# Four transformer layers on one core: the quantised layer's feed-forward in pieces over three attentions, and unread identity products on TensorE

## The chip, the cores and the metric

The kernel runs on one NeuronCore of one Trainium2 chip. The metric is the device time of one execution, in microseconds (us). Two kernels are compared by the median of their runs.

## The reference, cut to what matters

A batch of 16 sequences of 128 tokens with 256 features goes through four layers, one after the other. All arithmetic is in fp32 apart from the quantised products. Layer 1 is the one that the change touches:

```
def layer1(x, context):                       # 16 heads of 16 features, D = 256
    h1 = ln(x);  x = attn(h1, h1)      + x    # _attn below, deltas d_*1
    h2 = ln(x);  x = attn(h2, context) + x    # deltas d_*2
    h3 = ln(x);  a, g = split(h3 @ ff_w1 + ff_b1)          # ff_w1: 256 x 2048
    return a * gelu(g) @ ff_w2 + ff_b2 + x                 # ff_w2: 1024 x 256

def _attn(x, ctx):                            # fq: round to 8 bits, clip, scale back
    q, k, v = heads(x @ wq), heads(ctx @ wk), heads(ctx @ wv)
    attn = softmax(fq(q) @ fq(k).T * SCALE)
    return merge(fq(attn) @ fq(v)) @ wo + bo
```

Layer 0 has an attention over features and a feed-forward, layers 2 and 3 have two masked or plain attentions and a feed-forward each.

## The kernel before, in words

The 16 sequences are taken in four groups of four (g = 0 to 3). A group has two streams (st = 0, 1) of two sequences each. While one stream is in its attention, the other stream's projections, norms and feed-forward are issued between the steps of that attention. Every engine has its own in-order program; all are written out by the same planner, so the order on an engine is the order in the planner's lists.

An attention of a stream is 8 units of 4 heads x 128 queries x 128 keys. Function `attend` calls `together`, which runs 13 steps. In the quantised layer step i issues, on TensorE (PE): the score product of unit i (line 804, bf16, 512 columns), then the four transposes of unit i-4 (`turn`, line 816), then the value products of unit i-5 (`values`, line 831). VectorE (DVE) takes the row maxima of a unit's scores (lines 1191, 1193), ScalarE (ACT) the four exponentials (line 985), GpSimd (POOL) weighs and rounds them (line 1390); the transposed unit is copied back by DVE (units 0 to 3, line 1215) or ACT (units 4 to 7, line 976). Scores of unit u wait for the exponentials of unit u-2, because they share one of two PSUM banks; the transposes of unit u wait for POOL's rounding of it.

Each other piece of work has a slot, a step number, and is issued on PE right after that step's attention work; on the other engines one step later. The pieces of a stream in layer 1 are: `y` and `sum` (output projection and residual), `norm`, `scale`, `tin` (norm of x, transposed; ACT copies it to hT), `k`, `q`, `v` (projections: 4 matmuls each, then three DVE instructions that quantise, lines 1007, 1009, 1013), `keys` (POOL, line 1309), and the feed-forward: `f0` to `f7`, each 4 matmuls for one 128-wide chunk of both halves of ff_w1, a Gelu on ACT (line 942) and a product on DVE (line 1089) that writes a chunk of `hid`; then `y2`, 16 matmuls over `hid`, and `sum`. An fp32 matmul of the program is two records of the trace. PSUM banks 6 (`one`) and 7 (`other`) serve all these pieces; `f` alternates between them.

One pass of layer 1 runs four attentions: stream 1's first, stream 0's second, stream 1's second, stream 0's first of the next group. `joined_pass` puts the whole feed-forward of stream 0 into the third and that of stream 1 into the fourth, two chunks to a slot, with `y2` after them and the next group's `k`, `q`, `v` after `y2`. The slots run past the 13 steps, so these two attentions last longer than the other two. They are called the long attentions below, the others the short ones. Layers 0 and 1 use `joined_pass`, layers 2 and 3 `ahead_pass`.

Of the kernel before, what the change touches and what calls it, by code (L numbers as in the profile page):

```python
# [8 lines left out]
ACT = mybir.ActivationFunctionType  # L9
# [5 lines left out]
P = 128  # L15
C = D // P
G = 2
# [153 lines left out]
AHEAD_SLOT = {"stage": 0, "scale": 0, "ctx": 3, "tin": 3, "bias": 4, "k": 5, "q": 5, "v": 6, "keys": 10}  # L171
FIRST_AHEAD = 2
CLOSING_SLOT = {"ot": 0, "y": 1, "sum": 1, "norm": 2, "scale": 3, "post": 5, "tin": 7, "bias": 8}
LEFT_SLOT = {"sum": 1, "norm": 2, "scale": 4, "post": 6}
# [65 lines left out]
def program(nc, a, out):  # L240
    ctx = ExitStack()
    with ctx:
# [167 lines left out]
        def passes(eng, emit_mix, emit_piece, late, before_last=lambda layer: None):  # L410
# [31 lines left out]
            def joined_pass(layer, g, after, left):  # L442
# [10 lines left out]
                return left  # L453

            def ahead_pass(layer, g, after, left):
# [20 lines left out]
            left = []  # L476
            for layer in range(FIRST_AHEAD):
                for g in range(NG - 1):
                    left = joined_pass(layer, g, (layer, g + 1), left)
                before_last(layer)  # L480
                left = joined_pass(layer, NG - 1, (layer + 1, 0), left)
            for layer in range(FIRST_AHEAD, NL):
# [69 lines left out]
        LATE = 1  # L552
        SUM_LAG = 1
        KEYS_AHEAD = 3
        LOCAL_STEPS = {
# [28 lines left out]
        def _(pe):  # L584
# [12 lines left out]
            def emit_piece(layer, g, st, ahead=False, shift={}):  # L597
# [11 lines left out]

                def emit(piece, arg, n):  # L610
                    swapped = ahead or "early" in arg
                    if piece == "ctx":
                        if st == 1:

                            pe.wait_ge(c[0]["yadd_done"], G * use("yadd", layer, g, 0))
                        pe.wait_ge(q["ctx_loaded"], 16 * (use("ctx", layer, g, 0) + 1))
                        turned(one, ctx_in[st]).then_inc(q["ctx_ps"], 1)
# [138 lines left out]
            def emit_mix(kind, layer, g, st, arg, n, mix):  # L756
# [51 lines left out]
                def turn(u):  # L808
                    if quant:
                        pe.wait_ge(s["rounded"], U * phase("qatt", layer, g, mix, st) + u + 1)  # L810
                    else:
                        pe.wait_ge(s["exp_ready"], U * ap + u + 1)

                    pe.wait_ge(s["PT_ready"], U * ap + u - 1)
# [58 lines left out]
        def _(act):  # L873
            def emit_piece(layer, g, st, ahead=False, shift={}):
                q = c[st]
                due = partial(use_shifted, shift)
                target = hT_ahead[st] if ahead else hT[st]

                def emit(piece, arg, n):
                    swapped = ahead or "early" in arg  # L880
                    if piece == "ctx":
                        act.wait_ge(q["ctx_ps"], use("ctx", layer, g, 0) + 1)
                        act.activation(cT[st].rearrange("p c t -> p (c t)"), one, ACT.Copy).then_inc(q["ctx_ready"], 1)
                    elif piece == "stage":
# [10 lines left out]
                    elif piece == "tin":  # L895
                        act.wait_ge(q["tin_ps"], due("tin", layer, g, n["tin"]) + 1)
                        for m in range(C):
                            if arg:
# [33 lines left out]
                    elif piece[0] == "f":  # L932
                        f = int(piece[1:])
                        k = use("ffn", layer, g, n["ffn"])
                        b = one if f % 2 == 0 else other
                        if arg["act"] == "geglu":
# [63 lines left out]
        def _(dve):  # L1000
            def emit_piece(layer, g, st, ahead=False, shift={}):
# [12 lines left out]

                def emit(piece, arg, n):
                    swapped = ahead or "early" in arg
                    if piece == "norm":
                        k = due("norm", layer, g, n["norm"])

                        if n["yadd"]:  # L1020
                            dve.wait_ge(q["yadd_done"], G * use("yadd", layer, g, n["yadd"]))
                        else:
                            dve.wait_ge(q["yadd_done"], G * use("yadd", layer - 1, g + 1, 0))
# [17 lines left out]
                    elif piece == "sum":  # L1041
                        b = one if "act" in arg else other
                        dve.wait_ge(q["y_ps"], use("yadd", layer, g, n["yadd"]))
                        if "res" in arg:
# [17 lines left out]
                    elif piece in ("q", "k", "v") and "quant" in arg:  # L1062
# [4 lines left out]
                        if piece == "v":  # L1067
                            quantise(Vzb[st].rearrange("p g a x d -> p (g a) x d")[:, :, 0:4:3, :],
                                     O[st].rearrange("p g d -> p (g d)"), one if swapped else other, d, at, q["v_ready"], G)
                        else:  # L1070
                            dst, scratch, b = (QTb[st], QT[st], other if swapped else one) if piece == "q" else (KTb[st], KT[st], one if swapped else other)
                            quantise(dst.rearrange("p c t -> p (c t)"), scratch.rearrange("p c t -> p (c t)"), b, d, at,
                                     q[piece + "_ready"], C)
# [11 lines left out]
                    elif piece[0] == "f" and arg["act"] == "geglu":  # L1085
                        f = int(piece[1:])
                        b = one if f % 2 == 0 else other
                        dve.wait_ge(q["gate_ready"], FC * use("geglu", layer, g, 0) + f + 1)
# [380 lines left out]
```

## Time and profile before

| | |
|---|---|
| median of 3 runs | 1998.0 us (1997.23 to 1998.41) |
| profiled execution: its time | 2000.4 us |
| profiled execution: its span | 1998.7 us |
| PE / DVE / ACT / POOL busy | 1801.4 / 1275.4 / 1043.4 / 906.9 us |
| mean granted TensorE clock | 0.929 of 2.4 GHz |
| layer 1 from its second attention to layer 2's first score product | 357.6 to 933.2 us |

The page gives, for the slowest core, each engine's busy time over the span, and a strip in 40 slices with the busy tenths and the clock that TensorE was granted. A stretch can be asked for by itself; so can the chain of waits, which is followed back from the last instruction: at each step to what released it, or to the instruction before it on the same engine. Busy times of matmuls are modelled and overlap, so the distance from one start to the next, or the chain, says what a run of them costs.

### The profile page before, as it was taken

To read this page: it belongs to the slowest core of one execution; us is meant where nothing else is said; L and a number is where in the kernel's file an instruction comes from. 1 tells how busy PE (TensorE), PEld (TensorE's weight loads), DVE (VectorE), ACT (ScalarE), POOL (GpSimd) and SP (SyncE) were. 2 spreads that over 40 slices of the span, in tenths; PEclk is the share of its full clock that TensorE was granted. 3 is DMA by queue.
4 is the path that set the end of the run, shared out by engine and by line. 5 is a ranking of instruction groups with operands and counts; after the bars stand their busy time and mean duration, and the time that the engine had idled before them with its cause. 6 is when DMAs were issued, how large, how long until landed. Compare 5 with 4: busy or idle time off the path is not lost.

```text
span 1998.7 us, 34297 instructions
## 1 busy us (share of the span) xinstructions
PE 1801.4 (90%) x12225; PEld 1334.7 (67%) x12225; DVE 1275.4 (64%) x2286; ACT 1043.4 (52%) x3078; POOL 906.9 (45%) x1209
## 2 busy tenths in 40 slices
PE   4999888799889889889999999999999999999997
PEld 4787766466566656657767677676676676766766
DVE  5899996765665575574575756856646538365471
ACT  2222224565565475465565565655545656565662
POOL 5466555654463464463254444644444333333340
PEclk8999988788878878879999999999999999999999
DMA  7200000002000000000002000000000000000000
GB/s 228 92 10 6 11 6 6 1 6 90 1 6 6 1 6 6 1 6 6 1 7 90 1 7 6 6 7 1 7 6 2 12 1 7 22 7 1 12 1 11
DMA packets 31071, 35.63 MB, mean 18 GB/s; under 512 B 3164, under 2 KB 29752, under 8 KB 30520
## 3 DMA queue, kind: packets, MB, share of 16 engines
q1 hardware_dynamic: 30904, 33.44, 5.2%
q8 instruction: 100, 1.64, 0.3%
q14 instruction: 67, 0.55, 0.1%
HBM read 31.34 MB, written 2.10 MB: 17 GB/s over the span
## 4 chain that ended last, share of the span: by engine, by line
PE 59%; DVE 20%; ACT 11%; issue 6%; SPq 2%; DMA 1%; POOL 1%; DVEq 0%; ACTq 0%; POOLq 0%
PE ps L594 31%; PE ps L806 6%; PE ps L744 6%; PE ps L816 5%; PE ps L850 4%; ACT work L985 4%; DVE xn L1039 3%; ACT work L992 3%; DVE work L1185 3%; PE ps L607 2%; DVE rowmax L1189 2%; PE ps L766 1%; ACT hT L899 1%; DVE O L1228 1%; PE ps L831 1%
## 5 line engine op out<-in xcount | busy, mean ns | idle before, releaser
L594 PE MATMUL ps<-hT,w_slot 128*128 128x256 f32 x1696 | 413.7, 398 | 16.7 <-ACT hT L899 16.2
L1314 POOL TENSOR_TENSOR work<-KT,own_head 128x512 f32<-128x512 f32 x256 | 262.4, 1046 | 286.7 <-PE ps L806 179.7
L594 PEld LDWEIGHTS ps<-hT,w_slot 128*128 128x128 f32 x1696 | 326.2, 198 | 77.9 <-ACT hT L899 22.0
L992 ACT ACTIVATE work<-work,rowmax 128x128 f32<-128x128 f32 x768 | 246.1, 394 | 167.2 <-DVE rowmax L1189 166.5
L816 PEld LDWEIGHTS ps<-ident,work 128*128 128x128 f32 x1536 | 199.7, 153 | 170.6 <-issue 89.5
L985 ACT ACTIVATE work<-ps,rowmax,score_scale 128x128 f32<-128x128 f32 x512 | 228.7, 478 | 132.5 <-DVE rowmax L1193 132.0
L816 PE MATMUL ps<-ident,work 128*128 128x128 f32 x1536 | 266.3, 302 | 18.0 <-ACT work L992 17.2
L806 PE MATMUL ps<-work,QT 128*128 128x512 f32 x512 | 266.5, 605 | 9.9 <-POOL work L1314 4.9
L1390 POOL TENSOR_SCALAR work<-work,winv 128x128 f32<-128x128 f32 x512 | 185.5, 382 | 155.3 <-DVE winv L1205 153.1
L1228 DVE RECIPROCAL O<-ps 128x128 f32<-128x128 f32 x128 | 122.2, 955 | 176.4 <-PE ps L850 175.7
L978 ACT ACTIVATE work<-ps 128x512 f32<-128x512 f32 x256 | 151.0, 597 | 91.1 <-PE ps L816 90.4
L1330 POOL TENSOR_SCALAR vareps<-meanvar 128x2 f32<-128x2 f32 x88 | 19.4, 221 | 384.2 <-DVE meanvar L1032 381.1
L1061 DVE TENSOR_TENSOR x_all<-ps,x_all 128x512 f32<-128x512 f32 x72 | 49.6, 690 | 148.6 <-PE ps L594 83.9
L947 ACT ACTIVATE hid<-ps,vcols 128x256 f32<-128x256 f32 x192 | 80.8, 472 | 106.9 <-PE ps L594 106.7
L1189 DVE TENSOR_REDUCE rowmax<-work 128x4 f32<-128x512 f32 x192 | 131.7, 686 | 6.6
L1039 DVE TENSOR_SCALAR xn<-x_all,meanvar,rstd 128x256 f32<-128x256 f32 x176 | 128.5, 770 | 3.0 <-POOL rstd L1332 1.9
L1309 POOL TENSOR_TENSOR work<-QKb,own_quad 128x512 bf16<-128x512 bf16 x64 | 70.7, 1124 | 131.4 <-issue 125.8
L804 PE MATMUL ps<-work,QKb 64*128 64x512 bf16 x128 | 64.7, 511 | 63.7 <-ACT work L985 45.5
L594 PE MATMUL ps<-w_slot,OT 128*128 128x256 f32 x448 | 115.6, 404 | 6.0 <-ACT OT L931 4.8
L744 PE MATMUL ps<-w_slot,hid 128*128 128x256 f32 x512 | 116.5, 381 | 1.7 <-ACT hid L947 0.9
L985 ACT ACTIVATION_READ_ACCUMULATOR work<-ps,rowmax,score_scale 128x1 f32 x512 | 115.0, 225 | 0.0
L594 PE MATMUL ps<-w_slot,hid 128*128 128x256 f32 x512 | 113.2, 379 | 0.0
(132 smaller groups left out, 3112.0 us busy)
## 6 DMA issues: line engine op xcount, KB each, us to landing
ctx_in<-in_ctx SPq DMA_DIRECT2D x32, 256.0 KB, 2.7
w_slot<-in_L_xattn_W SPq DMA_DIRECT2D x2, 1024.0 KB, 6.3
w_slot<-in_L_xattn_ff_w SPq DMA_DIRECT2D x1, 2048.0 KB, 11.6
w_slot<-in_L_xattn_ffn_w SPq DMA_DIRECT2D x2, 1024.0 KB, 9.4
w_slot<-in_L_xattn_w SPq DMA_DIRECT2D x2, 1024.0 KB, 9.9
out<-x_all SPq DMA_DIRECT2D x8, 256.0 KB, 2.1
x_all<-in_x SPq DMA_DIRECT2D x1, 1536.0 KB, 12.9
pad<-in_mask_Bx1x1xS_fk SPq DMA_DIRECT2D x1, 1024.0 KB, 6.4
```

The lines of the kernel that those rows point to most:

```text
L594: mm = pe.matmul(dst, lhsT(k), rhs(k), start=(k == 0 and not onto), stop=(k == chunks - 1 and not more))
L744: mm = pe.matmul(one[:, j * D:(j + 1) * D], hid[:, k, tok(j)], w[arg["w2"]][:, k, :], start=(k == 0), stop=(k == FC - 1))
L806: pe.matmul(bank(u % 2), QT[st][:, m, tok(j)], KB[u % NK], start=True, stop=True).then_inc(s["scores_ps"], 1)
L816: mm = pe.transpose(bank(2 + u % 2)[:, tok(h)], prob[u % (NP if quant else NPF)][:, tok(h)], ident[:, :])
L978: act.activation(PTF[u % 4], bank(2 + u % 2), ACT.Copy).then_inc(s["PT_ready"], 1)
L985: ex = act.activation(prob[i % NP][:, tok(h)], bank(i % 2)[:, tok(h)], ACT.Exp, bias=shifts[:, at:at + 1], scale=score_scale[:, arg["quant ...
L992: ex = act.activation(prob[i % NPF][:, tok(h)], src[:, tok(h)], ACT.Exp, bias=shifts[:, at:at + 1])
L1039: dve.tensor_scalar(xn[st][:, j, :].unsqueeze(1), x_of(g, st, j), meanvar[st][:, j, 0:1], rstd[st][:, j:j + 1], ALU.subtract, ALU.mult).th ...
L1189: dve.tensor_reduce(shift_u, sc, AX.X, ALU.max, negate=True).then_inc(s["shift_ready"], 1)
L1228: dve.reciprocal(oinv[st][quarter], bank(4 + m)[:, sums_at:sums_at + S]).then_inc(s["oinv_ready"], 1)
L1314: pool.tensor_tensor(KB[u % NK].rearrange("p (h k) -> p h k", h=HU), keys, own_head[:, e:HC:2].unsqueeze(2).broadcast_to([P, HU, S]), ALU. ...
L1390: w = pool.tensor_scalar(prob[u % NP][:, tok(h)], prob[u % NP][:, tok(h)], winv[:, u // 2 % 2, at:at + 1], MAGIC, ALU.mult, ALU.add)
```

## The change: two edits

1. Layer 1 gets a pass of its own, `spread_pass`. The feed-forward of a stream is no longer in one attention. Its chunks f0 to f3 stand in one attention (slots 8 to 11, one to a slot), f4 to f7 in the next, and the 16 matmuls of `y2`, in four parts, at slots 0 to 3 of the third, with their `sum` at slot 4. The chunks use bank 6 alone, so a chunk's matmuls wait until DVE has read the chunk before; `k`, `q`, `v`, `tin` and `ctx` use bank 7 alone, so `q` waits for the quantised `k` and `v` for the quantised `q`. The next group's `k`, `q`, `v` stand at slots 7, 8, 9, inside the 13 steps. The last group of layer 1 keeps the joined form for its own feed-forward, and takes over what group 2 has left.
2. In every attention of layer 1 PE issues products of the identity with itself (`warm`, 128x128, fp32) into the PSUM bank of the next transposes, which nothing reads: 3, 6, 6 ahead of the score products of units 2, 3, 4, and 2, 3, 3, 3 ahead of the transposes of units 0 to 3. These are 26 per attention.

```diff
+SPREAD_START = {"tin": 3, "ctx": 4, "bias": 4, "k": 7, "q": 8, "v": 9, "keys": 9}
+SPREAD_NORM = {"norm": 8, "scale": 10}
+SPREAD_CLOSING = {"ot": 0, "y": 1, "sum": 1, "norm": 2, "scale": 4, "tin": 6, "bias": 8}
+SPREAD_HIDDEN = 8
+SPREAD_SUM = 4
+def spread_closing(layer):
+    hidden = [(SPREAD_HIDDEN + int(piece[1:]) % (FC // 2), piece, arg, n) ... if piece[0] == "f"]
+    product = [(part, f"y2{part}", pieces[y2][2], pieces[y2][3]) for part in range(Y2)]
+    return chain, hidden[:FC // 2], hidden[FC // 2:], product
...
+            def spread_pass(layer, g, after, left):
+                into_a, into_b, into_c = left
+                attend(layer, g, 1, 0, middle(0) + into_a)
+                if after[0] != layer:
+                    attend(layer, g, 0, 1, middle(1) + into_b)
+                    pieces, later = joined(layer, g, after, 0)
+                    attend(layer, g, 1, 1, [(p[0] // 2 if p[2] != "sum" else 1,) + p[1:] for p in into_c] + pieces)
+                    pieces, _ = joined(layer, g, after, 1)
+                    attend(*after, 0, 0, pieces + later)
+                    return []
+                attend(layer, g, 0, 1, middle(1) + start(0, SPREAD_NORM) + into_b)
+                chain_0, first_0, second_0, product_0 = end(0)
+                attend(layer, g, 1, 1, chain_0 + start(0, SPREAD_START) + first_0 + start(1, SPREAD_NORM) + into_c)
+                chain_1, first_1, second_1, product_1 = end(1)
+                attend(*after, 0, 0, chain_1 + start(1, SPREAD_START) + second_0)
+                return product_0 + first_1, second_1, product_1
...
+        WARM_SCORES = {2: 3, 3: 6, 4: 6}
+        WARM_TURNS = {0: 2, 1: 3, 2: 3, 3: 3}
...
+                    elif spread and piece in ("k", "q", "v"):
...
+                            pe.wait_ge(q["k_ready" if piece == "q" else "q_ready"], C * (use("att", layer, g, n["att"]) + 1))
...
+                    elif spread and piece[0] == "f":
...
+                            pe.wait_ge(q["hid_ready"], FC * use("ffn", layer, g, n["ffn"]) + f)
+                        product(one[:, 0:T], ...)
+                        product(one[:, T:2 * T], ...).then_inc(q["hid_ps"], 1)
...
+                def warm(u, count):
+                    pe.wait_ge(s["PT_ready"], U * ap + u - 1)
+                    for _ in range(count):
+                        pe.matmul(bank(2 + u % 2)[:, 0:P], ident[:, :], ident[:, :], start=True, stop=True)
...
+                    if quant and u in WARM_SCORES:
+                        warm(0, WARM_SCORES[u])
...
+                        warm(u, WARM_TURNS.get(u, 0))
```

How PE's program changes is seen best in its order. Before, a long attention: this is PE from the score product of unit 7 (L804) to the next attention's first scores. L594 x8 are two chunks `f` of stream 0 (hT0), L594 over `hid` x16 is `y2`, L607 turns the next group's input, and the last two L594 rows are `k`, `q` (x8) and `v` (x4).

```order
L804 MATMUL ps<-work,QKb1 128x512
L816 MATMUL ps<-ident,work 128x128 x4
L831 MATMUL ps<-work,V1 32x128 x4
L594 MATMUL ps<-hT0,w_slot1 128x256 x8
L816 MATMUL ps<-ident,work 128x128 x4
L831 MATMUL ps<-work,V1 32x128 x4
L594 MATMUL ps<-hT0,w_slot1 128x256 x8
```

and further down, from the last two chunks on:

```order
L594 MATMUL ps<-hT0,w_slot1 128x256 x8
L816 MATMUL ps<-ident,work 128x128 x4
L831 MATMUL ps<-below,V1 32x128 x4
L831 MATMUL ps<-work,V1 32x128 x4
L607 MATMUL ps<-ident,xn0 128x128 x4
L594 MATMUL ps<-w_slot1,hid 128x256 x16
L831 MATMUL ps<-below,V1 32x128 x4
L831 MATMUL ps<-work,V1 32x128 x4
L594 MATMUL ps<-hT0,w_slot1 128x256 x8
L594 MATMUL ps<-w_slot1,hT0 128x256 x4
L804 MATMUL ps<-work,QKb0 128x512 x2
```

After, the same part of an attention (here a pass's first, with stream 1's chunks): `k` (L653 over cT0), then `q` with the first chunk of hT1, `v` with the second, then one chunk to a step.

```order
L653 MATMUL ps<-cT0,w_slot1 128x256 x4
L927 MATMUL ps<-ident,work 128x128 x4
L942 MATMUL ps<-work,V1 32x128 x4
L653 MATMUL ps<-O0,w_slot1 128x256 x4
L653 MATMUL ps<-hT1,w_slot1 128x256 x4
L927 MATMUL ps<-ident,work 128x128 x4
L942 MATMUL ps<-below,V1 32x128 x4
L942 MATMUL ps<-work,V1 32x128 x4
L653 MATMUL ps<-w_slot1,cT0 128x256 x4
L653 MATMUL ps<-hT1,w_slot1 128x256 x4
L927 MATMUL ps<-ident,work 128x128 x4
```

Four chunks have come into an attention that had none, and `y2` has gone to the head of another. That head, before the change, on PE of a short attention (L594 over OT0 is `y`, L607 the turned context):

```order
L804 MATMUL ps<-work,QKb1 128x512 x2
L594 MATMUL ps<-w_slot1,OT0 128x256 x4
L804 MATMUL ps<-work,QKb1 128x512 x2
L607 MATMUL ps<-ident,ctx_in0 128x128 x4
L804 MATMUL ps<-work,QKb1 128x512
L816 MATMUL ps<-ident,work 128x128 x4
```

and after it, where L846 are the parts of `y2`, L893 the unread products and L914 the scores:

```order
L914 MATMUL ps<-work,QKb1 128x512
L846 MATMUL ps<-w_slot1,hid 128x256 x4
L914 MATMUL ps<-work,QKb1 128x512
L653 MATMUL ps<-w_slot1,OT0 128x256 x4
L846 MATMUL ps<-w_slot1,hid 128x256 x4
L893 MATMUL ps<-ident 128x128 x3
L914 MATMUL ps<-work,QKb1 128x512
L846 MATMUL ps<-w_slot1,hid 128x256 x4
L893 MATMUL ps<-ident 128x128 x6
L914 MATMUL ps<-work,QKb1 128x512
```

Between two score products that stood next to each other there are now up to 4 matmuls of `y2` and 6 unread products.

## Rows read from the trace of the kernel before

**Rows 1.** The page: the clock granted to TensorE, 40 equal slices
```profile
PEclk8999988788878878879999999999999999999999
```

**Rows 2.** Busy us by stretch: two short, a long, the last, layer 1; PEclk behind POOL
```profile
671.80:700.35 28.55, 23.65 (x125) 14.75 (x125) 21.41 (x48) 18.26 (x70) 18.03 (x40) 0.70 0.00 1
700.35:727.73 27.38, 22.68 (x128) 14.38 (x125) 20.69 (x47) 18.25 (x70) 18.35 (x41) 0.75 0.00 1
727.73:777.54 49.81, 45.59 (x233) 33.48 (x229) 25.75 (x61) 26.05 (x83) 20.52 (x44) 0.86 0.02 6
884.61:933.24 48.63, 45.12 (x233) 33.77 (x229) 20.02 (x48) 27.27 (x88) 19.18 (x41) 0.86 0.02 6
357.60:933.24 575.64, 503.51 (x2589) 351.54 (x2589) 349.41 (x789) 329.43 (x1146) 289.16 (x608) 0.81 0.04 11
```

**Rows 3.** The same view between two changes of the granted clock
```profile
640.90:672.90 32.00, 29.92 (x171) 24.26 (x169) 12.88 (x27) 9.34 (x16) 8.42 (x14) 1.00 0.01 2
672.90:690.00 17.10, 13.42 (x49) 7.14 (x50) 14.05 (x35) 14.06 (x61) 10.03 (x26) 0.56 0.00 0
```

**Rows 4.** Chain of waits, 652 to 672 us: start us, us, what
```profile
652.47 3.67 PE ps L594 x16
...
656.16 0.48 ACT gate L942
...
656.67 0.50 DVE hid L1089
...
657.87 6.91 PE ps L594 x32
...
665.11 1.94 PE ps L594 x8
...
667.07 0.76 DVE KT L1007
...
668.82 0.74 DVE QT L1007
...
670.67 1.07 DVE QKb L1013
```

**Rows 5.** Chain of waits, 672 to 702 us, a short attention
```profile
678.26 3.66 ACT work L985 x16
...
687.88 1.04 PE ps L816 x4
...
689.25 3.29 PE ps L594 x8
692.54 0.44 PE ps L816 x4
...
693.20 1.93 PE ps L594 x8
...
695.56 0.33 PE ps L831 x8
```

**Rows 6.** PE in order of time, a short attention's first score products [idle before <-releaser]
```profile
671.80 0.39 PE L804 MATMUL ps<-work,QKb 64*128 64x512 bf16 x1 [0.94 <-DVE QKb L1013]
673.51 0.39 PE L804 MATMUL ps<-work,QKb 64*128 64x512 bf16 x1 [1.33 <-DVE V L1013]
```

**Rows 7.** Chain of waits, 95 to 125 us: identity products of layer 0
```profile
94.94 2.90 PE ps L766 x26
```

**Rows 8.** ACT in order of time where Gelu follows Exp: start, us
```profile
639.79 0.27 ACT L985 ACTIVATION_READ_ACCUMULATOR work<-ps,rowmax,score_scale 128x1 f32 x1
640.08 1.28 ACT L942 ACT_TABLE_LOAD   x1
641.37 0.48 ACT L942 ACTIVATE gate<-ps,vcols 128x256 f32<-128x256 f32 x1
```

**Rows 9.** DVE groups, 463.57 to 777.5 us (two passes): xcount | busy, mean ns | idle before
```profile
L1191 DVE TENSOR_REDUCE rowmax<-ps 128x4 f32<-128x512 f32 x64 | 43.8, 685 | 7.0 <-PE ps L804 6.6 <-issue 0.3
L1193 DVE TENSOR_SCALAR rowmax<-rowmax,score_scale 128x4 f32<-128x4 f32 x64 | 17.1, 267 | 2.3
```

More of the change, by code:

```diff
@@ L172 @@
 FIRST_AHEAD = 2
+SPREAD = 1
+MIDDLE_SHIFT = {"yadd": -1}
+SPREAD_START = {"tin": 3, "ctx": 4, "bias": 4, "k": 7, "q": 8, "v": 9, "keys": 9}
[4 more added lines that the diff above has]
+def spread_closing(layer):
+    pieces = PLAN[layer][-1]
+    y2 = [piece for piece, _, _, _ in pieces].index("y2")
+    chain = [(SPREAD_CLOSING[piece], piece, arg, n) for piece, _, arg, n in pieces[:y2] if piece[0] != "f"]
+    hidden = [(SPREAD_HIDDEN + int(piece[1:]) % (FC // 2), piece, arg, n) for piece, _, arg, n in pieces[:y2] if piece[0] == "f"]
+    product = [(part, f"y2{part}", pieces[y2][2], pieces[y2][3]) for part in range(Y2)]
+    product.append((SPREAD_SUM,) + pieces[y2 + 1][0:1] + pieces[y2 + 1][2:])
+    return chain, hidden[:FC // 2], hidden[FC // 2:], product
 CLOSING_SLOT = {"ot": 0, "y": 1, "sum": 1, "norm": 2, "scale": 3, "post": 5, "tin": 7, "bias": 8}
@@ L453, in joined_pass, with middle, start, end @@
                 return left
+            def spread_pass(layer, g, after, left):
+                into_a, into_b, into_c = left
+                shift = MIDDLE_SHIFT if g else {}
+                def middle(st):
+                    emit = emit_piece(layer, g, st, "spread", shift)
+                    return [(spot, emit, piece, arg, n) for piece, spot, arg, n in PLAN[layer][2]]
+                def start(st, slots):
+                    emit = emit_piece(*after, st, "spread", {k: -v for k, v in ENDING[layer].items()})
+                    return [(slots[piece], emit, piece, arg, n) for piece, _, arg, n in PLAN[after[0]][0] if piece in slots]
+                def end(st):
+                    emit = emit_piece(layer, g, st, "spread", STARTING[layer])
+                    late_sum = emit_piece(layer, g, st, "spread", {**STARTING[layer], "yadd": 1})
+                    return [[(slot, late_sum if piece == "sum" and "act" in arg else emit, piece, arg, n) for slot, piece, arg, n in part]
+                            for part in spread_closing(layer)]
+                attend(layer, g, 1, 0, middle(0) + into_a)
[12 more added lines that the diff above has]
+                return product_0 + first_1, second_1, product_1
             def ahead_pass(layer, g, after, left):
@@ L476, in passes @@
             left = []
[L477 to L481, printed above, removed]
+            for g in range(NG - 1):
+                left = joined_pass(0, g, (0, g + 1), left)
+            before_last(0)
+            left = joined_pass(0, NG - 1, (1, 0), left), [], []
+            for g in range(NG - 1):
+                left = spread_pass(SPREAD, g, (SPREAD, g + 1), left)
+            before_last(SPREAD)
+            left = spread_pass(SPREAD, NG - 1, (SPREAD + 1, 0), left)
             for layer in range(FIRST_AHEAD, NL):
@@ L613, in emit @@
                         if st == 1:
                             pe.wait_ge(c[0]["yadd_done"], G * use("yadd", layer, g, 0))
+                        elif layer == SPREAD + 1 and g == 0:
+                            pe.wait_ge(c[1]["yadd_done"], G * use("yadd", SPREAD, NG - 1, 1))
                         pe.wait_ge(q["ctx_loaded"], 16 * (use("ctx", layer, g, 0) + 1))
@@ L882, in emit @@
                         act.wait_ge(q["ctx_ps"], use("ctx", layer, g, 0) + 1)
-                        act.activation(cT[st].rearrange("p c t -> p (c t)"), one, ACT.Copy).then_inc(q["ctx_ready"], 1)
+                        act.activation(cT[st].rearrange("p c t -> p (c t)"), other if spread else one, ACT.Copy).then_inc(q["ctx_ready"], 1)
                     elif piece == "stage":
@@ L896, in emit @@
                         act.wait_ge(q["tin_ps"], due("tin", layer, g, n["tin"]) + 1)
+                        target = hT_ahead[st] if ahead and not (spread and n["att"] == PER_PASS["att"][layer]) else hT[st]
                         for m in range(C):
@@ L934, in emit @@
                         k = use("ffn", layer, g, n["ffn"])
-                        b = one if f % 2 == 0 else other
+                        b = one if spread or f % 2 == 0 else other
                         if arg["act"] == "geglu":
@@ L1015, in emit @@
                 def emit(piece, arg, n):
+                    spread = ahead == "spread"
                     swapped = ahead or "early" in arg
@@ L1020, in emit @@
                         if n["yadd"]:
-                            dve.wait_ge(q["yadd_done"], G * use("yadd", layer, g, n["yadd"]))
+                            dve.wait_ge(q["yadd_done"], G * due("yadd", layer, g, n["yadd"]))
                         else:
@@ L1042, in emit @@
                         b = one if "act" in arg else other
-                        dve.wait_ge(q["y_ps"], use("yadd", layer, g, n["yadd"]))
+                        dve.wait_ge(q["y_ps"], due("yadd", layer, g, n["yadd"]))
                         if "res" in arg:
@@ L1086, in emit @@
                         f = int(piece[1:])
-                        b = one if f % 2 == 0 else other
+                        b = one if spread or f % 2 == 0 else other
                         dve.wait_ge(q["gate_ready"], FC * use("geglu", layer, g, 0) + f + 1)
```

44 lines of the change are left out of this document (39 added, 5 removed).

## The prediction

> **What bounds the kernel now.** I read the page's clock strip first. The reader is to see that TensorE has its full 2.4 GHz in layers 2 and 3 (slices 19 to 40), and falls short between slices 7 and 18 [rows 1]. That is layer 1, so I asked for the busy times of its attentions. A long attention takes 49.8 us with PE busy for 45.6; a short one takes 27.4 to 28.6 us, PE is idle for nearly 5 of them, and no other engine is busier than PE [rows 2]. Cut where the clock changes, it is 1.00 from the long attention's chunks on and 0.56 from the head of the short one to its first projection [rows 3]. TensorE has little to do while the first exponentials run, and afterwards runs at 1.2 GHz.
>
> The chain of waits says what ends each stretch. In a long attention it is PE at full clock: two feed-forward chunks, 16 records, take 3.67 us (1.83 a chunk), `y2` takes 6.91. Behind `y2` follow the projections and quantisations of the next group with PE mostly waiting: from 665.1 to 671.7 us, 6.6 us [rows 4]. In a head it is the exponentials, 3.66 us for two units (1.83 each). The half clock costs least there: four transposes 1.04 us against 0.44, a projection 3.29 against 1.93 [rows 5], about 2.5 to 4 us in an attention.
>
> **The change, part by part.** From the second attention of layer 1 to layer 2's first score product there are 15 attentions and 575.6 us [rows 2]. After the change they are of four kinds. C: two short ones without chunks (group 0). A: seven with four chunks. B: five with four chunks and a `y2` at their head. And the last one in the joined form, which also gets a `y2`. Nothing before or behind is moved; the first attention of layer 1 gets the unread products only, and I put that at nothing.
>
> Unread products. Their nearest row is the identity product of the same shape in layer 0: 26 records in 2.90 us, 0.112 each, 0.223 for a product of two records [rows 7]. 26 per attention are 5.8 us of PE. From below the cost is nothing, where PE would wait anyway, or a gain through the clock; from above it is that of 1.2 GHz, times 1.04/0.44 = 2.4 as for transposes, 0.53 each [rows 5]. I take 0.223, since with them PE has little idle time left and full clock is what PE has wherever it is this busy [rows 3].
>
> Head of kind A. A unit's first exponential starts 1.5 us after its score product begins: 0.39 for the product [rows 6], 0.69 and 0.27 on DVE [rows 9], the rest handoffs. Unit 7's score product waits for unit 5's exponentials: 1.5 + 6 x 1.83 = 12.5 us. PE's own work until there is 8 score products of at most 0.39, `y` 1.93, 23 unread products 5.1, three sets of transposes 1.3, values and a turned input about 1.1: 12.5 us at most. So both fit, and the unread products are hidden here. Exponentials of unit 6 end at 1.5 + 7 x 1.83 = 14.3, some 0.75 later since norms and row maxima meet on DVE; then ACT copies hT (1.1 us) and `k` can start at 16.2.
>
> Tail of kind A, at full clock: k 1.93, transposes and values 0.77 (0.44 + 0.33) [rows 5], a wait of 1.0 until `k` is quantised (1.75 us, 667.07 to 668.82 [rows 4], of which 0.77 is covered), q 1.93, chunk 1.83, 0.77, v 1.93, chunk 1.83, then twice 0.77, a wait of 0.35 and a chunk 1.83, and the last values 0.33. The 0.35 is what one bank costs: a chunk's Gelu and product take 1.07 us with their handoffs before the next may start, 656.14 to 657.17 [rows 4], and 0.77 of it is covered. Sum 18.2, so kind A takes 34.4 us. Before, two banks hid that round trip.
>
> Kind B adds 6.91 us for `y2` in the head, a quarter each behind the first four score products. Together with the unread products this is 13.3 us of PE until unit 4's scores are out (5 scores 1.1, `y` 1.9, `y2` 6.9, 15 unread 3.4), against 8.8 by the exponentials; unit 6's exponentials then end about 5 us later than in A. Kind B takes 39.4. Kind C is A without chunks, its waits for quantised `k` and `q` no longer covered (1.0 and 1.5): 16.2 + 11.7 = 27.9. The last takes 48.6 now [rows 2] and about 4 more for its `y2` head: 52.6.
>
> Sum: 2 x 27.9 + 7 x 34.4 + 5 x 39.4 + 52.6 = 546.2 us against 575.6, a gain of 29.4. The profiled execution would go from 2000.4 to 1971.0; it lay 2.4 above the median, so from 1998.0 I come to 1969. Where it comes from: a pass loses two exposed projection chains (13 us) and most of its half-clock time, and pays 23 us for unread products, of which about half is hidden.
>
> Further edits. DVE, ACT and POOL do the same instructions in other places. DVE is busy some 24 us in an attention on average [rows 2], below 34, so it hides, but its order matters: a chunk's product on DVE stands behind the quantisation of `q` or `v` (1.75 to 2.9 us; the longer one is 668.82 to 671.74 [rows 4]). In my tail the two end within 0.3 us of each other. DMAs are the same and small.
>
> Gelu and Exp now alternate in 12 attentions instead of 6 or so: by the order of ACT 12 more table loads. The row shows one at 1.28 us, starting 0.02 us after the last exponential's read and followed at once by the Gelu [rows 8]. The load ahead of the first Gelu lies under `k` and `q`. The one ahead of the next Exp starts 0.55 us after the last chunk and ends 1.85 after it; the first exponential is due 1.9 after it (0.33 values, 1.5). So I charge nothing.
> The Trainium skill, page "ScalarE: Activation LUTs", section "What ACT_TABLE_LOAD costs", puts a switch at 1283 ns for the load and some 1380 ns of drain. By that, an estimate from the page, each kind A would start its exponentials 1.3 us later and the time would be 9 us more, 1978. The load's length agrees with the trace, the drain has no gap there, and I go by the trace.
>
> **The rivals.**
> Better: the waits overlap better than I string them. Kind A has 34.4 - 29 = 5.4 us of waits, B about 3.3, by the sums above. If half goes, 7 x 2.7 + 5 x 1.7 = 27 us more, 1942. For it: in a long attention PE runs its chunks with no gap [rows 4]. Against it: the round trip and the quantised `q` are chains by data.
> Slower: the clock still falls in the heads. The mechanism is that a fall doubles what PE works on there, and in B (and in A with the unread products) PE is the bound of the head, which it is not today. For it: today's heads have PE busy 13.4 of 17.1 us and still show 0.56 [rows 3], and in the steps of units 5 to 7 exponentials keep PE waiting after the change too. Layer 1 has 0.19 x 2 x 575.6 = 219 us at 1.2 GHz now [rows 2]. Each us left at 1.2 GHz in a PE-bound stretch costs half a us, so from 59 us left the gain is gone, and with half of today's, 110 us, it is 55 - 29 = 26 us slower, 2024. Against it: at half clock the added products alone would keep PE busy without a gap, and with real products, which is the state in which it has the full clock [rows 3].
> No change: the one bank costs more than its 0.35. Three round trips in each of 12 attentions: with 0.8 us more each (a chunk's product stuck behind a quantisation or a norm on DVE) the 29 us are gone, 1998.
> The change not doing what it says would show as unread products late in the head, behind the exponentials; it is part of the case above.
>
> **How the numbers follow.** Forecast 0.52, its own range 1952 to 1990 (a us more or less in each of 15 attentions, and the table loads). Better 0.22. No change 0.09. Slower 0.17. A measurement of this kernel tells 0.2%, 4 us, from no change. Faster is 0.52 + 0.22 and a part of the third, 0.75; same 0.08; slower 0.17. The range that leaves out 2 in 10 goes from 1938, a little beyond the better case, to 2001, with most of the slower case outside.
>
> **What would show it.** The clock strip at 9 through slices 8 to 19. PE starts of attention heads some 34 and 39 us apart by turns, 27 to 28 for the first two. Waits of chunks for `hid` of a third of a us, of `q` for quantised `k` of one us, no exposed 6.6 us stretch. The exponentials of kind A with gaps under 1 us, those of units 2 to 4 in kind B with gaps of about 1.5. I am wrong if kind A is over 36.5 us, if the clock of layer 1 is below 0.9, or if attention heads with `y2` run over 22 us.

## The result

| | before | after |
|---|---|---|
| median of 20 runs each, same chips | 1998.34 us (1996.85 to 2000.56) | 2001.45 us (2000.20 to 2010.04) |
| profiled execution: time / span | 2000.4 / 1998.7 us | 2001.4 / 1999.7 us |
| mean granted TensorE clock | 0.929 | 0.988 |
| layer 1, second attention to layer 2's first score product | 575.6 us | 580.5 us |

The ratio after to before is 1.0023, interval 1.0014 to 1.0032. It is a ratio of means, and four of the 20 runs of after took 2009.4 to 2010.0 us; by the medians the change costs 3.1 us, 0.16%. The change makes the kernel about 0.2% slower. The forecast was 1969 us, 1.5% faster, and the range ended at 2001, half a microsecond short of the measured median.

The page of after, with the clock strip that answers to [rows 1]:

```profile
PE 1812.0 (91%) x13057; PEld 1389.3 (69%) x13057; DVE 1268.4 (63%) x2286; ACT 1054.7 (53%) x3090; POOL 904.3 (45%) x1209
...
PEclk8999989999999999999999999999999999999999
...
L893 PE MATMUL ps<-ident 128*128 128x128 f32 x832 | 119.3, 285 | 0.0
```

The clock is where it was wanted: every slice of layer 1 is at 9, where most were at 7 and 8. The time did not follow. The view by stretch, as in [rows 2], shows a B, the A behind it, and all of layer 1:

```profile
645.75:687.19 41.44, 38.25 (x245) 30.16 (x242) 21.56 (x51) 22.84 (x77) 17.93 (x39) 1.00 0.00 1
687.19:722.73 35.54, 30.97 (x212) 24.07 (x208) 24.24 (x56) 22.52 (x77) 18.99 (x41) 1.00 0.00 1
...
353.98:934.49 580.51, 516.54 (x3368) 404.75 (x3369) 343.01 (x789) 343.49 (x1158) 286.79 (x608) 1.00 0.04 12
```

TensorE's clock is 1.00 over the whole stretch (0.81 in [rows 2]), and the stretch is 4.9 us longer. PE is busy 516.5 of 580.5 us, so 64 us are still waits. What they wait for has changed. This is the view of PE's waits over layer 1, first of after, then of before (engine, line, what it waited for: us in total, times, longest):

```profile
PE ps L653 <- DVE QKb L1125: 20.2, 16, 2.5
...
PE ps L653 <- DVE hid L1202: 11.1, 25, 1.0
...
PE ps L914 <- ACT work L1097: 6.5, 18, 1.0
```

```profile
PE ps L804 <- ACT work L985: 42.8, 45, 1.6
```

The score products hardly wait for exponentials any more (42.8 to 6.5 us). In their place projections and chunks wait for DVE to free the one bank that each kind has: 20.2 us for a quantised `k` or `q` and 11.1 us for `hid`. In order of time these waits look like this: a `q` behind the quantised `k`, a `y` for OT at an attention's start, because DVE still has the last chunk's product to do, and the third chunk behind `hid`.

```profile
672.63 1.99 PE L653 MATMUL ps<-O,w_slot 128*128 128x256 f32 x8 [1.18 <-DVE QKb L1125]
...
688.40 1.99 PE L653 MATMUL ps<-w_slot,OT 128*128 128x256 f32 x8 [0.82 <-DVE OT L1332]
...
717.40 1.99 PE L653 MATMUL ps<-hT,w_slot 128*128 128x256 f32 x8 [0.95 <-DVE hid L1202]
```

The head of a kind B, in the chain of waits:

```profile
656.78 0.32 PE ps L914
657.10 1.92 PE ps L846 x8
659.02 1.34 PE ps L893 x12
...
664.96 1.88 ACT work L1097 x8
```

`y2` (L846) and the unread products (L893) stand in the chain one behind the other: 1.34 us for 6 products, 0.112 a record, as priced from [rows 7]. In this head the unread products are on the path, as the working for kind B had counted them.

### The profile page after: what moved, and what is told of

The parts are those of the page before. It is cut to its first block, busy times and chain, and to the rows that moved or that the text cites. A ratio compares the mean times of both kernels' runs of the same rounds, so it can differ in the third digit from the quotient of the medians.

```text
span 1999.7 us, 35908 instructions
## 1 busy us (share of the span) xinstructions
PE 1812.0 (91%) x13057; PEld 1389.3 (69%) x13057; DVE 1268.4 (63%) x2286; ACT 1054.7 (53%) x3090; POOL 904.3 (45%) x1209
## 4 chain that ended last, share of the span: by engine, by line
PE 61%; DVE 20%; ACT 12%; issue 6%; POOL 1%; DMA 0%; SPq 0%; DVEq 0%; ACTq 0%; POOLq 0%
PE ps L653 32%; PE ps L846 8%; PE ps L916 6%; PE ps L961 4%; ACT work L1097 4%; PE ps L927 3%; ACT work L1104 3%; DVE xn L1152 3%; DVE work L1298 3%; PE ps L868 3%; PE ps L893 2%; DVE rowmax L1302 2%; ACT hT L1011 2%; PE ps L666 1%; DVE O L1268 1%
## 5 line engine op out<-in xcount | busy, mean ns | idle before, releaser
L653 PE MATMUL ps<-hT,w_slot 128*128 128x256 f32 x1536 | 367.6, 390 | 28.0 <-ACT hT L1011 16.1
L653 PEld LDWEIGHTS ps<-hT,w_slot 128*128 128x128 f32 x1536 | 288.3, 193 | 82.2 <-ACT hT L1011 21.7
L927 PEld LDWEIGHTS ps<-ident,work 128*128 128x128 f32 x1536 | 184.5, 141 | 141.9 <-issue 73.3
L927 PE MATMUL ps<-ident,work 128*128 128x128 f32 x1536 | 233.0, 275 | 17.6 <-ACT work L1104 17.2
L846 PE MATMUL ps<-w_slot,hid 128*128 128x256 f32 x704 | 163.1, 383 | 4.2 <-DVE hid L1202 2.6
L846 PEld LDWEIGHTS ps<-w_slot,hid 128*128 128x128 f32 x704 | 131.5, 190 | 35.2 <-ACT hid L1059 10.3
L653 PE MATMUL ps<-w_slot,OT 128*128 128x256 f32 x448 | 113.0, 397 | 12.3 <-DVE OT L1332 6.6
L1304 DVE TENSOR_REDUCE rowmax<-ps 128x4 f32<-128x512 f32 x128 | 87.6, 685 | 50.0 <-PE ps L914 48.8
L893 PE MATMUL ps<-ident 128*128 128x128 f32 x832 | 119.3, 285 | 0.0
L893 PEld LDWEIGHTS ps<-ident 128*128 128x128 f32 x832 | 103.4, 191 | 19.8 <-issue 18.4
L653 PEld LDWEIGHTS ps<-w_slot,OT 128*128 128x128 f32 x448 | 86.2, 197 | 43.8 <-issue 14.5
```

What stands on the lines that cost most here:

```text
L653: mm = pe.matmul(dst, lhsT(k), rhs(k), start=(k == 0 and not onto), stop=(k == chunks - 1 and not more))
L846: mm = pe.matmul(one[:, j * D:(j + 1) * D], hid[:, k, tok(j)], w[arg["w2"]][:, k, :], start=(k == 0), stop=(k == FC - 1))
L893: pe.matmul(bank(2 + u % 2)[:, 0:P], ident[:, :], ident[:, :], start=True, stop=True)
```

## The experiments

Fifteen kernels ran. Each ratio is to the kernel before, in runs on the same chip, with its 95% interval. The attention lengths come from the traces, start to start. Each expectation names its own theories; the question behind all of them is where the forecast 29 us went: into the unread products, or into the waits for the single banks, or never existed because the full clock was worth less.

### One half of the change at a time

The spread order without unread products:

```diff
-        WARM_SCORES = {2: 3, 3: 6, 4: 6}
-        WARM_TURNS = {0: 2, 1: 3, 2: 3, 3: 3}
+        WARM_SCORES = {}
+        WARM_TURNS = {}
```

> The spread feed-forward alone, no unread products. Theory P (the unread products are paid for on TensorE's path): with y2 in the head 15 of the 26 (3.4 us) go straight off six heads, and the time is 1975 to 1985 us even if some clock is lost. Theory K (they buy more clock than they cost): the granted clock of layer 1 falls back to about 0.8 to 0.85, y2 and the chunks run partly at 1.2 GHz, and the time is 2010 us or more.

Measured: 2015.95 us, 1.0087 (1.0074 to 1.0100), clock 0.941; layer 1 takes 591.9 us at 0.85. Spreading the feed-forward alone loses 17 us, as theory K had it.

The kernel before, with the unread products of the change and nothing else (the same two tables, `warm`, its two calls, and PE's wait for the copied transposes, which now stands in `warm`):

> The kernel before with the 26 unread products per attention, feed-forward as before. Theory P: the heads are bound by exponentials, so the products are hidden there, and full clock takes 2 to 3 us off each of 16 attentions: 1955 to 1970 us. The whole loss then lies with the spreading. Theory K says the same of the clock. Rival (the half clock cost nothing, since the exponentials bound the heads anyway): 1993 to 2003 us at a clock near 1.

Measured: 1985.51 us, 0.9933 (0.9921 to 0.9945), clock 0.983, between theory P and the rival. Two short attentions, a long one and all of layer 1, to be held against [rows 2]:

```profile
664.26:692.43 28.17, 25.61 (x177) 19.45 (x177) 21.07 (x48) 18.26 (x70) 18.00 (x40) 0.94 0.00 1
692.43:718.28 25.85, 24.04 (x181) 18.15 (x177) 20.66 (x47) 18.07 (x70) 18.37 (x41) 1.00 0.01 2
718.28:767.10 48.82, 46.34 (x284) 36.94 (x281) 25.55 (x61) 25.59 (x83) 20.51 (x44) 1.00 0.02 6
354.43:920.43 566.00, 527.01 (x3368) 412.08 (x3369) 344.10 (x789) 326.26 (x1146) 289.62 (x608) 0.98 0.04 12
```

The clock of layer 1 rises from 0.81 to 0.98, and the attentions become shorter by 0.4 us (28.55 to 28.17), 1.5 (27.38 to 25.85) and 1.0 (49.81 to 48.82). The other long attention of each pass becomes 0.1 us longer (51.30 to 51.42). Its waits for exponentials:

```profile
PE ps L814 <- ACT work L996: 7.3, 27, 0.3
```

These fell from 42.8 to 7.3 us, but layer 1 fell only from 575.6 to 566.0. The chain of waits says why. In the first of the short attentions above it runs through unread products (L793) three times, 3.42 us in all, while transposes (L827) and projections (L596) on it are back at full clock, 0.44 and 1.92 us where [rows 5] has 1.04 and 3.29:

```profile
669.59 1.03 PE ps L793 x6
...
670.94 1.53 PE ps L793 x12
...
681.18 0.86 PE ps L793 x6
682.04 0.44 PE ps L827 x4
...
682.70 1.92 PE ps L596 x8
```

Added up over layer 1, the chain of the kernel before has 354.0 us of PE. With the products it has 343.5, of which 49.8 (8.8%) are unread products, so real work on it fell by 60.3. That is an estimate of what the full clock took off the path, since the chain goes another way in places (18 us less of ACT, 22 us more of DVE and POOL). The products that bought the clock put most of it back. No run has the clock without the products, so the two are not separated by an experiment.

So the products give 0.67% and spreading costs 0.87% by itself; the two add up to 0.20%, and the change measures 0.23%. The halves add up within their intervals: on top of the products, spreading costs 0.90%, 18 us by the ratios (1.0023 less 0.9933) and 17 by the medians. Within layer 1 it is 14.5 us (566.0 to 580.5).

### Unread products in the heads with y2

First the 15 ahead of score products are left out where `y2` is in the head, in six attentions; then the 11 ahead of transposes too (the second pair of lines, in the second kernel only).

```diff
-                    if quant and u in WARM_SCORES:
+                    if quant and u in WARM_SCORES and not (st == 1 and g > 0):
...
-                        warm(u, WARM_TURNS.get(u, 0))
+                        warm(u, 0 if st == 1 and g > 0 else WARM_TURNS.get(u, 0))
```

> The change without the 15 unread products ahead of score products in the six attentions whose head has y2 (streams 1, groups 1 to 3). Theory P: 6 x 3.4 = 20 us less than the change, about 1981 us, clock unchanged since y2 keeps TensorE busy. Theory K: the clock falls in those heads after y2 and the time is 1995 us or more.

> The change without any unread product in these six attentions. Theory P: another 0 to 6 us less than with the 11 ahead of transposes left in (they partly fill waits), 1975 to 1981 us. Theory K: steps of units 5 to 7 have only transposes and bf16 products left, the clock falls there, and k, q and the first chunk run at 1.2 GHz: 5 to 15 us more than with them.

Measured: 1988.66 us, 0.9954 (0.9941 to 0.9966), clock 0.986 for the first; 1995.11 us, 0.9988 (0.9979 to 0.9998), clock 0.975 for the second. The 15 products cost 0.69%, 13.8 us by the ratios. By the traces that is 2.6 us in each of the five Bs (the one at 645.75 falls from 41.44 to 38.84) and 0.3 us in the last attention. Theory P is right about the clock, but its 20 us were too much. The other 11 earn their place, as theory K had it: without them it is 6.5 us slower again and the clock falls. So in these heads the 15 cost more than they give, where `y2` already keeps PE busy, and the 11 give more than they cost.

### The order of chunks and projections

In every spread attention the chunk of a step now goes ahead of `q` or `v` of the same step, on all engines. Of the five calls that change alike the fence shows one:

```diff
+            def chunks_first(pieces):
+                return [p for p in pieces if p[2][0] == "f"] + [p for p in pieces if p[2][0] != "f"]
...
-                attend(layer, g, 1, 0, middle(0) + into_a)
+                attend(layer, g, 1, 0, chunks_first(middle(0) + into_a))
...
```

> The change with one order swapped: at slots 8 and 9 the feed-forward chunk is issued ahead of q and of v instead of behind them. Theory W (the spreading loses by chains through one bank): q no longer waits 1.18 us for the quantised k, the third chunk no longer up to 0.95 us, in 12 attentions: 14 to 25 us less than the change, 1979 to 1989 us. Theory Y (it loses by y2 in the heads, and the tail's waits are covered by something else): 0 to 5 us less.

Measured: 1996.44 us, 0.9990 (0.9981 to 0.9999), 6.6 us less than the change by the ratios, between the two theories. Most attentions become shorter, as theory W has it: A falls from 35.54 to 33.27 and from 36.79 to 35.15 us, the B with 43.62 to 41.33. But the B with 41.44 rises to 43.80 and the last A from 34.91 to 37.19. In this B DVE, POOL and PE, in order of time:

```profile
670.27 3.31 DVE L1125 TENSOR_SCALAR QT<-QT 128x512 f32<-128x512 f32 x1
...
670.27 3.03 POOL L1426 TENSOR_TENSOR work<-QKb,own_quad 128x512 bf16<-128x512 bf16 x3
...
674.17 3.50 PE L657 MATMUL ps<-w_slot,cT 128*128 128x256 f32 x8 [2.04 <-DVE QKb L1129]
```

The reader sees one DVE instruction take 3.31 us, beside three of POOL that start at the same moment and take 3.03. Elsewhere the same instruction takes 0.43 us (663.35 in the trace of a kernel below). `v` waits 2.04 us for it, and then runs at half clock, 3.50 us where it takes 1.99.
The Trainium skill, page "SBUF — State Buffer", section "Who interferes with whom", says that DVE and GpSimd share a pair of SBUF ports as an exclusive lock, which a tensor_scalar can take in its two-port mode, and that the second to issue "fully blocks". The trace agrees in that DVE ends at 673.58, 0.28 us after POOL's third instruction at 673.30; that DVE did not come in between the three is this trace's alone.

Two slots later for `y2` and its sum (in the last attention one slot for `y2` and two for the sum), on the change itself, so that the first exponentials start ahead of it:

```diff
-SPREAD_SUM = 4
+SPREAD_SUM = 6
...
-    product = [(part, f"y2{part}", ...) for part in range(Y2)]
+    product = [(part + 2, f"y2{part}", ...) for part in range(Y2)]
```

> The change with the four parts of y2 at slots 2 to 5 instead of 0 to 3 (their sum at slot 6, in the last attention at 3), unread products as in the change. Theory Y: exponentials of units 2 to 4 start up to 3 us sooner in six heads, 6 to 15 us less than the change, 1988 to 1997 us. Theory W: the head is full of TensorE work anyway (y2 6.9 and products 3.4 us), the same work in another order, within 4 us of the change.

Measured: 1999.11 us, 1.0002 (0.9993 to 1.0011), 0.2% less than the change, at the edge of theory W; the Bs take 40.6 and 41.7 to 42.2 us, and the last attention grows from 55.0 to 57.1 us.

### Edits put together

Chunks first, no head products beside `y2`, and the double-banked order kept for group 0, which has no chunks (kind C); then `y2` later too:

```diff
-                    emit = emit_piece(layer, g, st, "spread", shift)
+                    emit = emit_piece(layer, g, st, "spread" if g else False, shift)
```

> Three parts: no products ahead of scores beside y2 (as the third run), chunks ahead of q and v (as e5), and in group 0, where no chunk is in flight, k, q, v in two banks as before the change. Theory W: the sum of the parts, -14 for the first (measured 0.9954 against 1.0023), -14 to -25 for the second, -4 for the third (28.2 and 31.9 us back to 25.9 and 30.0): 1958 to 1970 us. Theory Y: about 1980 us.

> As the run before it, and y2 at slots 2 to 5. Theory Y: with the products gone from these heads the exponentials bind again and the later y2 fills their gaps: another 5 to 8 us less. Theory W: within 3 us of the run before it.

Measured: 1976.15 us, 0.9888 (0.9874 to 0.9901), and 1971.42 us, 0.9863 (0.9849 to 0.9876). The first misses its expected 1958 to 1970: the swapped order had given 6.6 us by itself, not 14 or more. The second gains 4.7 us by the medians, just under what theory Y asks, and the two intervals touch.

On the second of these, chunks behind `k`, `q` and `v` again in the one kind of attention that had become longer; and then the last chunk of each four one slot later on ACT and DVE (on PE it stays):

```diff
-                attend(layer, g, 1, 0, chunks_first(middle(0) + into_a))
+                attend(layer, g, 1, 0, middle(0) + into_a)
```

```diff
+                def last_chunk_later(part):
+                    return [(p[0] + (1 if late and p[2] in ("f3", "f7") else 0),) + p[1:] for p in part]
```

> The eighth run, but in the attention of stream 1's first product (and in the last group's next one) q and v stand ahead of the chunks again, since there the swap cost 2.3 us (43.8 against 41.4 us, 37.2 against 34.9) while it gained 1.6 to 2.3 us elsewhere. Theory D (GpSimd's key products and DVE's quantisation of q meet there): 3 x 2.3 + 2.3 = 9 us less than the eighth run, 1962 us. Rival: the loss is only moved, 1969 to 1973 us.

> The ninth, and on DVE and ACT the last chunk of an attention stands behind DVE's copy of the attention's output, so that y does not wait for it (0.82 us, eight times in the change). If that wait is on the path: 4 to 7 us less than the ninth. If the exponentials of the next head cover it: within 2 us.

Measured: 1968.59 us, 0.9847 (0.9833 to 0.9861), and 1963.14 us, 0.9825 (0.9811 to 0.9838). The first gained 3 us by the medians where 9 were expected, and its interval overlaps that of the kernel it starts from: it only evades the meeting of POOL and DVE, and gives up the better order in that attention (its B takes 37.9 us, and 36.3 with the edit that follows below). The second gained 5.5 us by the medians, as expected if `y`'s wait is on the path, but the traces show 0.17 us in each of 11 attentions, about 2 us; the rest is not explained, and the intervals overlap.

### The keys of POOL behind the quantised q

The cause itself, taken away: POOL's first key product waits until DVE has quantised `q`. The edit is put on the chunks-first kernel, and on the best kernel with chunks first:

```diff
+                if u == 0 and quant:
+                    pool.wait_ge(q["q_ready"], C * (use("att", layer, g, n["att"]) + 1))
```

> The fifth run (chunks ahead of q and v) with one wait added: GpSimd starts the next attention's key products only when DVE has quantised q as well. Theory D: the second DVE instruction on q, 3.31 us there against 0.43 elsewhere, goes back to 0.43 and the attention of 43.8 us to 41 or less, and with three of these and the last group's 8 to 14 us go: 1983 to 1989 us. Rival (the 3.31 us has another cause, or the later keys delay the next first score product as much): 1994 to 2000 us.

> The eighth run with that wait. Theory D: 8 to 12 us less than the eighth, 1959 to 1963 us. Rival: 1969 us or more.

Measured: 1977.86 us, 0.9894 (0.9880 to 0.9908), 19 us less than without the wait and more than the 8 to 14 expected, and 1958.96 us, 0.9799 (0.9782 to 0.9815), 12 us less than its parent. In the first, the same two instructions:

```profile
663.35 0.43 DVE L1125 TENSOR_SCALAR QT<-QT 128x512 f32<-128x512 f32 x1
...
664.55 3.03 POOL L1428 TENSOR_TENSOR work<-QKb,own_quad 128x512 bf16<-128x512 bf16 x3 [1.17 <-DVE QKb L1129]
```

POOL waits 1.17 us and does its work as fast as before, DVE needs 0.43 us again. The three Bs of this kind fall from 43.80 to 39.80 and the last A from 37.19 to 33.27. That is more than the 2.9 us of the one instruction, since `v` behind it is at full clock again, 1.5 us. The traces have 16.0 us in layer 1, so some 3 of the 19 us lie elsewhere or in the spread of the runs.

Is this meeting also what made the change slow? The same wait on the change, and on the kernel before with unread products:

> The change itself, its order as it is, with only the wait of the key products for the quantised q. Theory Q (the change lost because the single bank makes q wait, and the meeting of GpSimd and DVE is a matter of the swapped order only): within 3 us of the change, 2000 to 2006 us, since DVE's instructions on q take 0.53 us on average there already. Rival (that meeting is part of the change's loss): 5 us less or more, 1998 us or below.

> The kernel before with unread products and with that wait. Theory Q: in the long attentions q is quantised 1.1 us sooner, but the key products, which the next scores need, start 2 us later: 0 to 10 us more than the products alone (1985.5 us). Rival: 3 us less or better.

Measured: 2001.88 us, 1.0015 (1.0006 to 1.0024), and 1988.99 us, 0.9943 (0.9930 to 0.9955). Neither differs from its parent (1.0023 and 0.9933) by more than the intervals allow, as theory Q had it. In the change `q` is quantised ahead of the chunks, and the instruction that took 3.31 us takes 0.64 us at most from 353.98 us on: the meeting is no part of the cause, and it appears only once the order is mended.

The last chunk late on the best kernel:

> The twelfth run with the last chunk behind the copy of the attention's output on DVE, as in the tenth, where it gave 0.17 us in each of 11 attentions: 1 to 3 us less than the twelfth, 1956 to 1958 us.

Measured: 1956.41 us, 0.9783 (0.9770 to 0.9796), 2.2% less than before and 2.4% less than after. This is the best version; its part over the kernel without the edit is within the intervals.

## Why the prediction was wrong

**What held.** The clock of layer 1 came back to 1.00, an unread product costs 0.112 a record, the attentions are of the forecast kinds, and the table loads stayed hidden. There are 26 instead of 14 in layer 1, the 12 more of the working. ACT at the start of an A:

```profile
686.96 0.47 ACT L1054 ACTIVATE gate<-ps,vcols 128x256 f32<-128x256 f32 x1 [1.90 <-PE ps L653]
687.45 1.28 ACT L1097 ACT_TABLE_LOAD   x1
689.24 0.46 ACT L1097 ACTIVATE work<-ps,rowmax,score_scale 128x128 f32<-128x128 f32 x1 [0.51 <-DVE rowmax L1306]
```

The load ends at 688.73, and the exponential waits another 0.51 us for its row maxima. So it is at the start of all twelve of these attentions.

**The sum did not hold.** Against 546.2 us the stretch took 580.5, 34.3 more:

| kind | predicted | measured | more |
|---|---|---|---|
| C, two | 2 x 27.9 | 31.9, 28.2 | 4.3 |
| A, seven | 7 x 34.4 = 240.8 | 34.9 to 38.1, in all 254.4 | 13.6 |
| B, five | 5 x 39.4 = 197 | three of 41.4, 43.1 and 43.6, in all 211.0 | 14.0 |
| the last | 52.6 | 55.0 | 2.4 |

Of the 27.6 us in A and B, 22.7 lie before `k` starts (A 10.4, B 12.3) and 4.9 behind it.

**The step that failed first: the head of the attentions, up to `k`.** The working put the end of unit 6's exponentials at 14.3 us and "some 0.75 later since norms and row maxima meet on DVE", then ACT's copy, and `k` at 16.2, the same for all A. In four of the seven, those that turn the input of a feed-forward and also the next group's input, it starts after 18.4 to 19.1 us. In the one at 766.35 unit 6's exponentials end at 17.3, which is 3.0 late and not 0.75. ACT copies the next group's input and context between the exponentials and then waits for row maxima that stand on DVE behind `xn`, the normalised input. At the end `k` waits 1.21 us until ACT has copied the feed-forward's input out of bank 7.

```profile
775.43 1.04 ACT L1011 ACTIVATE O<-ps,vcols 128x256 f32<-128x256 f32 x2
...
778.06 0.65 ACT L994 ACTIVATE cT<-ps 128x512 f32<-128x512 f32 x1
...
781.91 0.46 ACT L1097 ACTIVATE work<-ps,rowmax,score_scale 128x128 f32<-128x128 f32 x1 [1.44 <-DVE rowmax L1306]
...
783.67 1.02 ACT L1011 ACTIVATE hT<-ps,vcols 128x256 f32<-128x256 f32 x2
```

```profile
784.75 1.99 PE L653 MATMUL ps<-O,w_slot 128*128 128x256 f32 x8 [1.21 <-ACT hT L1011]
```

In the other three A `k` starts at 16.5, close to the 16.2 of the working, but that is luck: unit 5's exponentials end at 14.5 instead of 12.5, behind a gap of 1.56 us at 699.86, and in return ACT's copy stands ahead of unit 6's exponentials, not behind them, so that `k` waits for nothing.

**The second: the head of B.** The working rightly had PE bound there and charged the 15 unread products at 3.4 us; in the chain they take 3.35. But its 13.3 us to the end of unit 4's scores are 14.9: `y2` in four parts takes 7.6 us in the chain and not 6.91, and its first part waits 0.43 us for `hid`. "About 5 us later than in A" became 6.5, and `k` starts 23.05 us after the head's start in three Bs and 24.6 in the two that turn both inputs, not 21.2. Leaving the 15 products out gives 2.6 us a head back; that was a cost known to the sum, and avoidable.

**The third, and small: the single banks.** `q` waits 1.18 us for the quantised `k` where 1.0 stood, in all twelve. The third chunk waits 0.95 us for `hid` where 0.35 stood in four of them, because its product lies on DVE behind the three instructions that quantise `v` (the working saw the two end "within 0.3 us of each other" and charged nothing); the others wait 0.3 to 0.4. `y` waits 0.82 for OT behind the last chunk's product, which was not in the sum; where it was taken away it gave 0.17 us an attention. C is 4.3 us over in all, most of it in the first, where `k` starts at 18.3 and `q` waits 2.5 us. With chunks ahead of `q` and `v` and the wait on POOL layer 1 took 22.5 us less, and A 33.3 to 35.8; most of what that gained are waits that the sum had charged.

**What the full clock is worth** was no term of the sum, whose kinds are strung at full clock. "About 2.5 to 4 us in an attention" and "pays 23 us for unread products, of which about half is hidden" stood in the account of where the gain comes from. By the chains the kernel with the products alone has 60.3 us less real work of PE on its path in 15 attentions, an estimate of 4 us in each, and the products put 49.8 us back on it, 3.3 in each. In the feed-forward's old place that leaves 9.6 us of 575.6, for 219 us at 1.2 GHz.

**The signs.** Of the signs of being wrong two are there: four of the seven A are over 36.5 us, and heads with `y2` run over 22. A third sign, gaps under 1 us between the exponentials of A, did not come: they go up to 1.6 us.

**The rivals.** "No change: the one bank costs more than its 0.35" (0.09) has nearly the time that came, 1998, but by luck: it needs 0.8 us more at each of 36 round trips, and there are 0.6 more at four. "Slower: the clock still falls in the heads" has the right sign by a wrong cause: the clock does not fall. I had no rival in which the exponentials of the last units come late and `k` with them, though the rows for it were there: in [rows 2] PE idles nearly 5 us in a short attention, and the kernel before has the same wait for row maxima behind a norm, in the attention at 671.80:

```profile
685.11 0.46 ACT L985 ACTIVATE work<-ps,rowmax,score_scale 128x128 f32<-128x128 f32 x1 [1.34 <-DVE rowmax L1193]
```

What stays open: why DVE could not start between the three POOL instructions of the keys, and what the head would take with the norm and ACT's copies in other slots, which no run tried. That they make `k` late is read from the trace of the change and is not tested. Chunks in two banks inside the spread order were not tried either.

## What to carry to other kernels

Unread work that keeps a clock up is itself work on the path: price both. Here the full clock took some 60 us of real work off the path, by an estimate from the chains, and the products put 50 back. Where other work already keeps the engine busy they only cost. A head that is "bound by exponentials" is also bound by everything that stands between them: copies on the same engine, and norms ahead of their row maxima on another. Read the gaps of the last units from the trace instead of multiplying the first ones. Work that is moved into another engine's idle time brings its buffers with it; if it loses its second buffer on the way, each hand-over becomes a wait, and which of two pieces goes first in a step decides how long it is. After mending one order, read the durations again: an instruction that grows from 0.4 to 3.3 us has met another engine, and a wait put on the one with time to spare can be worth more than the change itself.

## What the runs showed of the hardware

- A DVE instruction of 0.43 us (128x512, fp32, SBUF to SBUF) took 3.31 us beside three GpSimd products of 3.03 us in all. Making GpSimd wait 1.17 us gave 19 us in the kernel as a whole, at four such meetings; part of it is that PE ran at a clock of 0.57 from 674 to 678 us, behind its wait, in the chunks-first kernel.
- The granted clock of a stretch went from 0.81 to 0.98 with 9.6 of 575.6 us as the gain, because the unread products that raised it took 49.8 us of the chain of waits.
- 26 instead of 14 switches between the Gelu and the Exp tables cost nothing that the trace shows: at twelve attention starts the exponential waits 0.5 us more for its row maxima after the load has ended.
